# One order for five engines, rewritten: a pipelined two-layer gated block on one core

## Chip, core and metric

One NeuronCore of a Trainium2 chip runs the whole program. The metric is the device time of one execution in microseconds. The engines are named as in the profile: PE (TensorE, matmuls; PEld is its weight load), DVE (VectorE), ACT (ScalarE), POOL (GpSimd) and SP (SyncE, which only issues DMAs here).

## What is computed

64 samples of `x` (256 rows of 256) go through two gated cross-attention blocks and two gated feed-forward blocks against a context of 120 rows. All in float32. Products with a split operand are done in three fp32r passes (hi by hi, hi by lo, lo by hi).

```python
x = x + tanh(g_xattn[0]) * L0_xattn(ctx, ctx, layernorm(x))   # A: softmax over the 16 heads
x = x + tanh(g_ffn[0])   * L0_ffn(layernorm(x))               # B: silu(gate) * up, then down
x = x + tanh(g_xattn[1]) * L1_xattn(layernorm(x), ctx)        # C: one key/value head, softmax over keys
x = x + tanh(g_ffn[1])   * L1_ffn(layernorm(x))               # D: one 256x256 product with a bias
```

## The kernel before

The four steps are called A, B, C and D. A sample goes through all of them in seven loop passes: pass t makes the layernorm and transposes of A for sample t, the scores of A for t-1 and t-2, B for t-3, C over the passes behind that and D for t-6. So six passes lie in a straight-line front, 58 in a hardware loop `Fori` on each of the five engines, and six in a straight-line tail. The order of instructions on every engine is written out by hand, one list an engine, and what passes between engines is ordered by semaphores (`wait_ge` before, `then_inc` behind an instruction); each counts one up a pass.

What comes on PE in a pass, and what each writes: `scores0(c)` the scores of A for one half c of the queries, into the four `scores` banks of PSUM; `key_scores(c)` the scores of C from which only the maxima are taken, `scores1(cc)` those of C with the maxima subtracted, both into the same four banks; `attended0`, `attended1` the sums over values; `transposes(bank, st)` the transposed layernorm of step st; `queries`, `keys0`, `values0`, `keys_values1` the projections; `rows_out` the output products `wo0` (A), `wo1` (C) and `f1` (D); `gate_up(bank, m)` and `down(bank, m)` the six slices of B. All but the scores go through four work banks W[0] to W[3], one PSUM bank each, and every writer waits for the last reader of its bank. `keep_busy(bank, n)` issues n matmuls whose result nobody reads, fillers for stretches in which PE waits; they stand in the front and the tail only.

What hangs on them: DVE takes `head_max(c)` over the scores, subtracts it in two halves (`subtract_max`), ACT makes the two exponentials, POOL adds the heads (`add_heads`, `heads_total`, the last result is `z`), DVE takes `reciprocal0` and multiplies (`normalise`). `key_max(c)` on DVE makes the maxima of C; PE transposes them, ACT copies them to `mT`, and four small DMAs (`maxima_rows`) bring them into `qm1`, for which `scores1(0)` waits (`max_rows`). For B, ACT makes `tanh(m)`, DVE `gated(m)` and `hidden(m)` into two alternating buffers, ACT `hidden_hi(m)`, POOL `hidden_lo(m)`. For C, DVE's `queries_to_rows`, `reciprocal1`, `weigh` and `queries_to_columns` lead from `attended1` to `y1f`, split by ACT (`yC_hi`) and POOL (`yC_lo`). A layernorm is `moments` on DVE (two statistics, a wait for them, a small copy, two aggregates), `root` on POOL (four instructions, the last writes `shift`), `ln_apply` on ACT (two), `transposes` on PE, a copy and a rounding on ACT, and the low part on POOL or DVE.

The order on PE in a pass of the loop before: wo1, queries C, down 3 to 5, key_scores(1), transposes D, wo0, values0, key_scores(0), queries A, f1, transposes B, scores0(1), maxima, keys0, transposes A, gate_up 0 to 2, scores1(0), gate_up 3 and 4, scores1(1), attended1(0), gate_up 5, scores0(0), attended1(1), attended0 twice, transposes C, down 0 and 1, keys_values1, down 2 (lines 2460 to 2531). DVE's loop begins between the two subtractions of c=0 (line 1782). The lines that the prediction names: L1488, L1491, L1493 the parts of `moments`; L1517 `head_max`; L1523 `subtract_max`; L1511 `hidden`; L1531 `reciprocal0`; L1538 `queries_to_rows`; L402 to L408 `root`; L857 the exponentials; L814 `ln_apply`; L2175 transposes; L2218 `key_scores`; L2229 `scores0`; L2239 `scores1`; L2278 fillers.

## Times and profile before

| | |
|---|---|
| median of 3 runs | 2446.68 us (2445.35 to 2448.39) |
| profiled execution, its span | 2442.8 us |
| busy share of the span | PE 97%, DVE 90%, POOL 73%, ACT 70% |
| granted TensorE clock, mean | 0.996 |
| DMA | 73.26 MB, 30 GB/s |

The span is the time from the first to the last instruction of one profiled execution. A busy share is an average over the whole; where an engine waits, and for whom, is read in the timeline, which lists instructions with start, duration and, in square brackets, the idle time before them and what ended it. Matmuls overlap, so the time of a block of them is best read from one start to the next.

### The profile page before, as it was taken

The page shows a single profiled execution, that of the slowest core. Times are in us where ns is not written, and L with a number is a line of the kernel's source. Part 1 is how long each engine was busy: PE and PEld are TensorE (multiplying, and loading weights), DVE is VectorE, ACT ScalarE, POOL GpSimd, SP SyncE. Part 2 cuts the span into 40 slices and gives each one's busy share as a digit, 9 for nine tenths or more (in the row PEclk, how much of TensorE's full clock was granted, in tenths as well). Part 3 has the DMA queues.
Part 4 walks back from the last instruction along what each step waited for, and adds up shares of the span by engine and source line. Part 5 has one row for each costly group of instructions (what it writes and reads, how often), then busy time and mean ns, then how long its engine had stood idle before and what let it go on. Part 6 is the DMA issues. An engine that isn't in the chain of part 4 may idle for free.

```text
span 2442.8 us, 70142 instructions
## 1 busy us (share of the span) xinstructions
PE 2357.7 (97%) x27814; PEld 2081.6 (85%) x27814; DVE 2205.6 (90%) x3678; ACT 1719.5 (70%) x3402; POOL 1773.4 (73%) x2512
## 2 busy tenths in 40 slices
PE   6899999999999999999999999999999999999897
PEld 5788888888888888888888888888888888888786
DVE  6879999999999999999999999999999999999963
ACT  4567777777777777777777777777777777777664
POOL 3667777777777777787777777777777777777653
PEclk9999999999999999999999999999999999999999
DMA  3000010010011010011001000001001001101000
GB/s 106 25 19 29 28 35 24 28 35 24 28 35 30 22 35 30 26 31 30 28 28 30 28 28 31 28 28 35 24 28 35 24 28 35 30 22 35 17 19 15
DMA packets 74326, 73.26 MB, mean 30 GB/s; under 512 B 6555, under 2 KB 73393, under 8 KB 74290
## 3 DMA queue, kind: packets, MB, share of 16 engines
q1 hardware_dynamic: 74290, 72.75, 9.5%
q8 instruction: 26, 0.43, 0.1%
q14 instruction: 10, 0.08, 0.0%
HBM read 54.90 MB, written 16.78 MB: 29 GB/s over the span
## 4 chain that ended last, share of the span: by engine, by line
PE 64%; DVE 19%; ACT 7%; POOL 7%; issue 2%; DMA 0%; POOLq 0%; SPq 0%; DVEq 0%; ACTq 0%
PE work L2136 13%; PE work L2137 11%; PE work L2138 11%; DVE m L1517 6%; PE scores L2229 6%; PE scores L2239 5%; PE work L2272 5%; PE work L2175 4%; DVE scores L1523 4%; ACT e L857 3%; POOL zt L417 3%; PE scores L2218 3%; ACT xn_D L814 3%; PE work L2153 2%; PE work L2159 2%
## 5 line engine op out<-in xcount | busy, mean ns | idle before, releaser
L857 ACT ACTIVATE e<-scores 120x1024 f32<-120x1024 f32 x512 | 513.4, 1029 | 88.3 <-PE scores L2239 56.6
L2136 PE MATMUL work<-xt_hi_B,w_hi 128*128 128x256 f32 x1536 | 456.5, 297 | 3.8 <-DVE y_lo_A L1497 1.6
L2137 PE MATMUL work<-xt_lo_B,w_hi 128*128 128x256 f32 x1536 | 430.2, 280 | 0.0
L2138 PE MATMUL work<-xt_hi_B,w_lo 128*128 128x256 f32 x1536 | 430.0, 280 | 0.0
L417 POOL TENSOR_TENSOR zt<-e 120x512 f32<-120x512 f32 x256 | 328.7, 1285 | 118.1 <-ACT e L857 112.1
L411 POOL TENSOR_TENSOR h_lo<-h_f,h_hi 128x256 fp32r<-128x256 f32 x384 | 279.5, 735 | 147.3 <-ACT h_hi L807 147.1
L1517 DVE TENSOR_REDUCE m<-scores 120x128 fp32r<-120x2048 f32 x128 | 291.0, 2273 | 66.2 <-PE scores L2229 66.0
L2136 PEld LDWEIGHTS work<-xt_hi_B,w_hi 128*128 128x128 f32 x1536 | 289.3, 188 | 60.6 <-DVE h_f L1511 24.9
L1523 DVE TENSOR_TENSOR scores<-scores,m 120x1024 f32<-120x1024 f32 x256 | 302.8, 1227 | 4.3
L1535 DVE TENSOR_TENSOR e<-e,work 120x2048 f32<-120x2048 f32 x128 | 291.4, 2277 | 0.2
L2137 PEld LDWEIGHTS work<-xt_lo_B,w_hi 128*128 128x128 f32 x1536 | 289.9, 189 | 0.0
L2138 PEld LDWEIGHTS work<-xt_hi_B,w_lo 128*128 128x128 f32 x1536 | 289.3, 188 | 0.0
L1526 DVE TENSOR_REDUCE m<-scores 128x16 f32<-128x1920 f32 x128 | 275.4, 2152 | 5.8 <-PE scores L2218 4.9
L807 ACT ACTIVATE h_hi<-h_f 128x256 fp32r<-128x256 f32 x384 | 160.6, 419 | 132.1 <-DVE h_f L1511 131.8
L2136 PE MATMUL work<-w_hi,h_hi 128*128 128x256 f32 x768 | 224.3, 292 | 0.6 <-DVE x L1554 0.6
L2137 PE MATMUL work<-w_lo,h_hi 128*128 128x256 f32 x768 | 213.2, 278 | 0.0
L2138 PE MATMUL work<-w_hi,h_lo 128*128 128x256 f32 x768 | 212.9, 277 | 0.0
L607 POOL TENSOR_TENSOR y_lo_C<-y1f,y_hi_C 128x512 fp32r<-128x512 f32 x58 | 73.9, 1274 | 165.6 <-ACT y_hi_C L807 165.6
L814 ACT ACTIVATE xn_B<-x,shift_B,rstd_B 128x256 f32<-128x256 f32 x128 | 70.1, 595 | 158.8 <-POOL shift_B L408 158.8
L851 ACT ACTIVATE th<-work 128x256 f32<-128x256 f32 x384 | 150.7, 393 | 31.3 <-PE work L2138 14.2
L1508 DVE SCALAR_TENSOR_TENSOR act_g<-th,work 128x256 f32<-128x256 f32 x384 | 157.3, 410 | 9.9 <-ACT th L851 9.8
L421 POOL TENSOR_TENSOR zt<-zt 120x512 f32<-120x512 f32 x128 | 165.4, 1292 | 0.8
(256 smaller groups left out, 7283.5 us busy)
## 6 DMA issues: line engine op xcount, KB each, us to landing
x_ln<-xp SPq DMA_DIRECT2D x64, 256.0 KB, 2.7
x_res<-xp SPq DMA_DIRECT2D x64, 256.0 KB, 2.7
y<-y_out SPq DMA_DIRECT2D x64, 256.0 KB, 2.2
ctx_f_A<-cp SPq DMA_DIRECT2D x64, 128.0 KB, 2.5
ctx_f_C<-cp SPq DMA_DIRECT2D x64, 128.0 KB, 2.0
qm<-mT SPq DMA_DIRECT2D x256, 4.0 KB
e<-wi SPq DMA_DIRECT2D x3, 768.0 KB, 5.5
w_ctx<-wc SPq DMA_DIRECT2D x1, 656.0 KB
```

Source lines behind the costliest of these rows:

```text
L411: return pool.tensor_tensor(h_lo[:, m, :], h_f[:, m % 2, :], h_hi[:, m, :].bitcast(F32), ALU.subtract)
L417: return pool.tensor_tensor(zt[0:SC, c, 4 * h:4 * h + 4, :], e0[0:SC, c, 2 * h, :, :], e0[0:SC, c, 2 * h + 1, :, :], ALU.add)
L421: pool.tensor_tensor(zt[0:SC, c, 0:4, :], zt[0:SC, c, 0:4, :], zt[0:SC, c, 4:8, :], ALU.add)\
L807: return act.activation(out, src, ACT.Copy)
L857: return act.activation(e[0:SC, c, 2 * h:2 * h + 2, :, :].rearrange("p a b n -> p (a b n)"), scores[0:SC, 2 * h:2 * h + 2, :].rearrange("p ...
L1517: return dve.tensor_reduce(m0[0:SC, c, :], scores[0:SC, :, :].rearrange("p r (h n) -> p n (r h)", n=P), AX.X, ALU.max)
L1523: return dve.tensor_tensor(banks, banks, row, ALU.subtract)
L1526: return dve.tensor_reduce(m1[:, c, :].rearrange("p (r x) -> p r x", r=RG)[:, :, 0:4], scores[:, :, :].rearrange("p r (h n) -> p r h n", n ...
L1535: return dve.tensor_tensor(e, e, bank[0:SC, 0:P].unsqueeze(1).to_broadcast([SC, H, P]), ALU.mult)
L2136: pe.matmul(out, a_hi, b_hi_, start=first, stop=False, skip_group_check=parts)
L2137: pe.matmul(out, a_hi, b_lo_, start=False, stop=False, skip_group_check=parts)
L2138: last = pe.matmul(out, a_lo, b_hi_, start=False, stop=end, skip_group_check=parts)
```

## The change

All five orders are rewritten, in the front, in the loop and in the tail. The work is the same: the same products, the same elementwise instructions, the same 58 passes in the loop. What differs:

- The loop begins at another place of the cycle: on PE at `scores1(1)` instead of `wo1`, on DVE at `gated(3)`, on ACT at `tanh(4)`, on POOL at `hidden_lo(3)`. The front ends there and the tail begins there.
- `moments` is split into `bn_moments` and `aggregate`, each with its place in the order. For C the aggregates come after the next `head_max(1)`; the small copy reads `ident` instead of the statistics, and for C it is left out.
- The blocks of a pass use other work banks, so other bank waits stand before them.
- On SP the two loads of x stand together at the start of a pass, and `load_ctx("C")` behind `load_ctx("A")`.
- Fillers: 137 in the front and 121 in the tail before; 97 and 188 after. All but one group of the tail write a work bank that holds nothing in use.

The loops of before are printed above. Of the diff, this is the split and the five new loops (ACT's in part), then the end of PE's tail:

```diff
-DEPTH = 6
+LEAD = 6
+TAIL = 0
...
-            def moments(st, x, t):
-                for i in range(NT):
-                    last = dve.bn_stats(stats[st][:, i, :], x[:, i, :])
-                last.then_inc(s[f"ln_mom_{st}"], 1)
-                dve.wait_ge(s[f"ln_mom_{st}"], within(0, 1, t))
-                dve.tensor_copy(ln_count[:, :], stats[st][:, 0, 0:1])
-                for i in range(NT):
-                    last = dve.bn_aggr(mv[st][:, i, :], stats[st][:, i, :])
-                return last
+            def bn_moments(st, x):
+                for i in range(NT):
+                    last = dve.bn_stats(stats[st][:, i, :], x[:, i, :])
+                return last
+
+            def aggregate(st):
+                for i in range(NT):
+                    last = dve.bn_aggr(mv[st][:, i, :], stats[st][:, i, :])
+                return last
...
+with nc.sync.Fori(FIRST + LEAD, LAST + 1 - TAIL) as t:
+    load_x_ln(t)
+    load_x_res(t - 3)
+    sp.wait_ge(s["v0_mm"], t)
+    load_ctx("A", t - 1)
+    load_ctx("C", t - 4)
+    sp.wait_ge(s["mT_out"], t)
+    maxima_rows()
+    sp.wait_ge(s["res_D"], t)
+    store_y(t - 6)
...
+with nc.gpsimd.Fori(FIRST + LEAD, LAST + 1 - TAIL) as t:
+    pool.wait_ge(s["G_hi"], nth(3, 6, t - 1))
+    hidden_lo(3).then_inc(s["G_lo"], 1)
+    pool.wait_ge(s["yC_hi"], t)
+    pool.tensor_tensor(y_lo["C"][:, :, :], y1f[:, :, :], y_hi["C"][:, :, :].bitcast(F32), ALU.subtract)\
+    .then_inc(s["yC_lo"], 1)
+    pool.wait_ge(s["G_hi"], nth(4, 6, t - 1))
+    hidden_lo(4).then_inc(s["G_lo"], 1)
+    pool.wait_ge(s["T_hi_C"], t)
+    pool.tensor_tensor(xt_lo["C"][:, :, :], xt["C"][:, :, :], xt_hi["C"][:, :, :].bitcast(F32), ALU.subtract)\
+    .then_inc(s["T_lo_C"], 1)
+    hidden_lo(5).then_inc(s["G_lo"], 1)
+    pool.wait_ge(s["ln_eps_D"], t)
+    root("D", t - 6).then_inc(s["ln_rstd_D"], 1)
+    pool.wait_ge(s["ld_x_res"], 16 * t)
+    add_row(x_res, x_res, 0).then_inc(s["dn_add_res"], 1)
+    pool.wait_ge(s["A0_exp"], 2 * t)
+    add_heads(0, 1).then_inc(s["A0_zb"], 1)
+    pool.wait_ge(s["ln_eps_A"], t)
+    root("A", t).then_inc(s["ln_rstd_A"], 1)
+    pool.wait_ge(s["T_hi_D"], t)
+    pool.tensor_tensor(xt_lo["D"][:, :, :], xt["D"][:, :, :], xt_hi["D"][:, :, :].bitcast(F32), ALU.subtract)\
+    .then_inc(s["T_lo_D"], 1)
+    pool.wait_ge(s["ln_eps_B"], t)
+    root("B", t - 3).then_inc(s["ln_rstd_B"], 1)
+    add_heads(0, 0).then_inc(s["dn_heads_00"], 1)
+    pool.wait_ge(s["T_hi_B"], t)
+    pool.tensor_tensor(xt_lo["B"][:, :, :], xt["B"][:, :, :], xt_hi["B"][:, :, :].bitcast(F32), ALU.subtract)\
+    .then_inc(s["T_lo_B"], 1)
+    pool.wait_ge(s["dn_heads_00"], t)
+    heads_total(0, t - 2).then_inc(s["A0_z"], 1)
+    pool.wait_ge(s["A1_exp"], nth(0, 2, t))
+    add_heads(1, 0)
+    pool.wait_ge(s["A1_exp"], 2 * t)
+    add_heads(1, 1).then_inc(s["A1_zb"], 1)
+    pool.wait_ge(s["G_hi"], nth(0, 6, t))
+    hidden_lo(0).then_inc(s["G_lo"], 1)
+    pool.wait_ge(s["A1_zb"], t)
+    heads_total(1, t - 2).then_inc(s["A1_z"], 1)
+    pool.wait_ge(s["G_hi"], nth(1, 6, t))
+    hidden_lo(1).then_inc(s["G_lo"], 1)
+    pool.wait_ge(s["G_hi"], nth(2, 6, t))
+    hidden_lo(2).then_inc(s["G_lo"], 1)
+    add_row(x3_biased, x3, 1).then_inc(s["dn_add_x3"], 1)
+    root("C", t - 4).then_inc(s["ln_rstd_C"], 1)
+    pool.wait_ge(s["dn_add_x3"], t)
+    last_residual(x3_biased).then_inc(s["res_D"], 1)
...
+with nc.scalar.Fori(FIRST + LEAD, LAST + 1 - TAIL) as t:
+    act.wait_ge(s["G_mm"], nth(4, 6, t - 1))
+    tanh(4, W[3]).then_inc(s["G_tanh"], 1)
...
+    values1_out(W[1]).then_inc(s["dn_v1_out"], 1)
+    act.wait_ge(s["T_mm_C"], t)
+    act.activation(xt["C"][:, :, :], two(W[0], KC), ACT.Copy).then_inc(s["T_out_C"], 1)
+    keys1_even(W[1]).then_inc(s["dn_k1_even"], 1)
+    hidden_hi(4).then_inc(s["G_hi"], 1)
+    hidden_hi(5).then_inc(s["G_hi"], 1)
+    act.wait_ge(s["T_out_C"], t)
+    split_hi(xt_hi["C"][:, :, :], xt["C"][:, :, :]).then_inc(s["T_hi_C"], 1)
+    keys1_odd(W[1]).then_inc(s["kz1_odd"], 1)
+    act.wait_ge(s["A0_sub_dve"], nth(0, 2, t))
+    exponential(e0, 0, 0).then_inc(s["A0_exp"], 1)
+    act.wait_ge(s["A0_sub_dve"], 2 * t)
+    exponential(e0, 0, 1).then_inc(s["A0_exp"], 1)
+    split_hi(y_hi["A"][:, :, :], two(W[3], KC)).then_inc(s["yA_hi"], 1)
+    act.wait_ge(s["res_C"], t)
+    act.activation(x2_before[:, :, :], x2[:, :, :], ACT.Copy).then_inc(s["x2_before"], 1)
+    act.wait_ge(s["q_mm_C"], t)
+    query_out("C", W[1]).then_inc(s["q_out_C"], 1)
+    act.wait_ge(s["ln_rstd_D"], t)
+    ln_apply("D", x3).then_inc(s["ln_D"], 1)
...
+with nc.vector.Fori(FIRST + LEAD, LAST + 1 - TAIL) as t:
+    dve.wait_ge(s["G_tanh"], nth(3, 6, t - 1))
+    dve.wait_ge(s["G_h"], nth(1, 6, t - 1))
+    gated(3, W[0]).then_inc(s["G_a"], 1)
+    dve.wait_ge(s["A1_z"], t - 1)
+    dve.wait_ge(s["G_h"], nth(2, 6, t - 1))
+    reciprocal0(W[2], 1).then_inc(s["A1_rz"], 1)
+    dve.wait_ge(s["G_tanh"], nth(4, 6, t - 1))
+    gated(4, W[3]).then_inc(s["G_a"], 1)
+    dve.wait_ge(s["G_a"], nth(3, 6, t - 1))
+    dve.wait_ge(s["G_lo"], nth(1, 6, t - 1))
+    hidden(3, W[0]).then_inc(s["G_h"], 1)
+    dve.wait_ge(s["G_a"], nth(4, 6, t - 1))
+    dve.wait_ge(s["G_lo"], nth(2, 6, t - 1))
+    hidden(4, W[3]).then_inc(s["G_h"], 1)
+    dve.wait_ge(s["yz0_mm"], t)
+    queries_to_rows(0, W[1]).then_inc(s["yz0"], 1)
+    normalise(W[2], 1).then_inc(s["A1_p"], 1)
+    dve.wait_ge(s["yz1_mm"], t)
+    queries_to_rows(1, W[1]).then_inc(s["yz1"], 1)
+    dve.wait_ge(s["G_tanh"], 6 * (t - 1))
+    gated(5, W[0]).then_inc(s["G_a"], 1)
+    dve.wait_ge(s["yz1"], t)
+    reciprocal1().then_inc(s["rz1"], 1)
+    dve.wait_ge(s["G_a"], 6 * (t - 1))
+    dve.wait_ge(s["G_lo"], nth(3, 6, t - 1))
+    hidden(5, W[0]).then_inc(s["G_h"], 1)
+    dve.wait_ge(s["rz1"], t)
+    weigh().then_inc(s["y_weighed"], 1)
+    dve.wait_ge(s["y_weighed"], t)
+    queries_to_columns().then_inc(s["yC"], 1)
+    dve.wait_ge(s["A0_mm"], t)
+    head_max(0).then_inc(s["A0_max"], 1)
+    dve.wait_ge(s["A0_max"], t)
+    subtract_max(0, 0).then_inc(s["A0_sub_dve"], 1)
+    subtract_max(0, 1).then_inc(s["A0_sub_dve"], 1)
+    dve.wait_ge(s["woC_mm"], t)
+    residual(x3, x2_before, W[0]).then_inc(s["res_C"], 1)
+    dve.wait_ge(s["res_C"], t)
+    bn_moments("D", x3).then_inc(s["ln_mom_D"], 1)
+    dve.wait_ge(s["ln_mom_D"], t)
+    dve.tensor_copy(ln_count[:, :], ident[:, 0:1])
+    aggregate("D").then_inc(s["ln_eps_D"], 1)
+    dve.wait_ge(s["yA_hi"], t)
+    low(y_lo["A"][:, :, :], two(W[3], KC), y_hi["A"][:, :, :]).then_inc(s["yA_lo"], 1)
+    dve.wait_ge(s["ld_x_ln"], 16 * t)
+    bn_moments("A", x_ln).then_inc(s["ln_mom_A"], 1)
+    dve.wait_ge(s["ln_mom_A"], t)
+    dve.tensor_copy(ln_count[:, :], ident[:, 0:1])
+    aggregate("A").then_inc(s["ln_eps_A"], 1)
+    dve.wait_ge(s["x2_before"], t)
+    dve.wait_ge(s["dn_mm"], 6 * t)
+    residual(x2, x1, W[2]).then_inc(s["res_B"], 1)
+    dve.wait_ge(s["M1_mm"], t)
+    key_max(1).then_inc(s["M1_max"], 1)
+    dve.wait_ge(s["dn_add_res"], t)
+    dve.wait_ge(s["res_B"], t)
+    dve.wait_ge(s["woA_mm"], t)
+    residual(x1, x_res, W[1]).then_inc(s["res_A"], 1)
+    dve.wait_ge(s["res_A"], t)
+    bn_moments("B", x1).then_inc(s["ln_mom_B"], 1)
+    dve.wait_ge(s["ln_mom_B"], t)
+    dve.tensor_copy(ln_count[:, :], ident[:, 0:1])
+    aggregate("B").then_inc(s["ln_eps_B"], 1)
+    dve.wait_ge(s["M0_mm"], t)
+    key_max(0).then_inc(s["M0_max"], 1)
+    bn_moments("C", x2).then_inc(s["ln_mom_C"], 1)
+    dve.wait_ge(s["v0_mm"], t)
+    values0_out(W[1]).then_inc(s["v0_pad"], 1)
+    dve.wait_ge(s["A1_mm"], t)
+    dve.wait_ge(s["ln_mom_C"], t)
+    head_max(1).then_inc(s["A1_max"], 1)
+    aggregate("C").then_inc(s["ln_eps_C"], 1)
+    dve.wait_ge(s["A1_max"], t)
+    subtract_max(1, 0).then_inc(s["A1_sub_dve"], 1)
+    subtract_max(1, 1).then_inc(s["A1_sub_dve"], 1)
+    dve.wait_ge(s["G_tanh"], nth(0, 6, t))
+    gated(0, W[0]).then_inc(s["G_a"], 1)
+    transposed_lo("A", W[1]).then_inc(s["T_lo_A"], 1)
+    dve.wait_ge(s["G_a"], nth(0, 6, t))
+    hidden(0, W[0]).then_inc(s["G_h"], 1)
+    dve.wait_ge(s["A0_z"], t)
+    dve.wait_ge(s["T_lo_A"], t)
+    reciprocal0(W[1], 0).then_inc(s["A0_rz"], 1)
+    dve.wait_ge(s["G_tanh"], nth(1, 6, t))
+    gated(1, W[3]).then_inc(s["G_a"], 1)
+    dve.wait_ge(s["G_tanh"], nth(2, 6, t))
+    gated(2, W[2]).then_inc(s["G_a"], 1)
+    dve.wait_ge(s["G_a"], nth(1, 6, t))
+    hidden(1, W[3]).then_inc(s["G_h"], 1)
+    normalise(W[1], 0).then_inc(s["A0_p"], 1)
+    dve.wait_ge(s["G_a"], nth(2, 6, t))
+    dve.wait_ge(s["G_lo"], nth(0, 6, t))
+    hidden(2, W[2]).then_inc(s["G_h"], 1)
...
+with nc.tensor.Fori(FIRST + LEAD, LAST + 1 - TAIL) as t:
+    pe.wait_ge(s["T0_exp"], 2 * (t - 1))
+    scores1(1).then_inc(s["T1_mm"], 1)
+    pe.wait_ge(s["A0_p"], t - 1)
+    attended1(W[1], 0).then_inc(s["yz0_mm"], 1)
+    pe.wait_ge(s["G_h"], nth(3, 6, t - 1))
+    gate_up(W[0], 5).then_inc(s["G_mm"], 1)
+    pe.wait_ge(s["T1_exp"], 2 * t)
+    pe.wait_ge(s["yz0"], t)
+    attended1(W[1], 1).then_inc(s["yz1_mm"], 1)
+    attended0(W[3], 0).then_inc(s["yA0_mm"], 1)
+    scores0(0).then_inc(s["A0_mm"], 1)
+    pe.wait_ge(s["A1_p"], t)
+    attended0(W[3], 1).then_inc(s["yA1_mm"], 1)
+    pe.wait_ge(s["ld_ctx_C"], 16 * (t - 1))
+    pe.wait_ge(s["yz1"], t)
+    keys_values1(W[1]).then_inc(s["kv1_mm"], 1)
+    pe.wait_ge(s["ln_C"], t)
+    pe.wait_ge(s["G_h"], 6 * (t - 1))
+    transposes(W[0], "C").then_inc(s["T_mm_C"], 1)
+    down(W[2], 0).then_inc(s["dn_mm"], 1)
+    down(W[2], 1).then_inc(s["dn_mm"], 1)
+    pe.wait_ge(s["T_out_C"], t)
+    pe.wait_ge(s["yC_lo"], t)
+    rows_out(W[0], y_hi["C"], y_lo["C"], "wo1", False).then_inc(s["woC_mm"], 1)
+    down(W[2], 2).then_inc(s["dn_mm"], 1)
+    down(W[2], 3).then_inc(s["dn_mm"], 1)
+    pe.wait_ge(s["kz1_odd"], t)
+    pe.wait_ge(s["T_lo_C"], t)
+    queries(W[1], "C", "q1", False).then_inc(s["q_mm_C"], 1)
+    down(W[2], 4).then_inc(s["dn_mm"], 1)
+    pe.wait_ge(s["G_lo"], 6 * (t - 1))
+    down(W[2], 5).then_inc(s["dn_mm"], 1)
+    pe.wait_ge(s["q_out_C"], t)
+    key_scores(1).then_inc(s["M1_mm"], 1)
+    pe.wait_ge(s["ln_D"], t)
+    pe.wait_ge(s["yA_lo"], t)
+    transposes(W[3], "D").then_inc(s["T_mm_D"], 1)
+    rows_out(W[1], y_hi["A"], y_lo["A"], "wo0", False).then_inc(s["woA_mm"], 1)
+    pe.wait_ge(s["T_out_D"], t)
+    queries(W[3], "A", "q0", False).then_inc(s["q_mm_A"], 1)
+    pe.wait_ge(s["M1_max"], t)
+    key_scores(0).then_inc(s["M0_mm"], 1)
+    pe.wait_ge(s["res_A"], t)
+    values0(W[1]).then_inc(s["v0_mm"], 1)
+    pe.wait_ge(s["T_lo_D"], t)
+    rows_out(W[2], xt_hi["D"], xt_lo["D"], "f1", False).then_inc(s["f1_mm"], 1)
+    pe.wait_ge(s["ln_B"], t)
+    transposes(W[0], "B").then_inc(s["T_mm_B"], 1)
+    pe.wait_ge(s["M0_max"], t)
+    scores0(1).then_inc(s["A1_mm"], 1)
+    pe.wait_ge(s["T_out_B"], t)
+    maxima_transposed(W[0]).then_inc(s["mT_mm"], 1)
+    pe.wait_ge(s["ld_ctx_A"], 16 * t)
+    keys0(W[2]).then_inc(s["k0_mm"], 1)
+    pe.wait_ge(s["v0_pad"], t)
+    transposes(W[1], "A").then_inc(s["T_mm_A"], 1)
+    pe.wait_ge(s["mT_out"], t)
+    pe.wait_ge(s["T_lo_B"], t)
+    gate_up(W[0], 0).then_inc(s["G_mm"], 1)
+    pe.wait_ge(s["q_out_A"], t)
+    gate_up(W[3], 1).then_inc(s["G_mm"], 1)
+    pe.wait_ge(s["kz0_odd"], t)
+    gate_up(W[2], 2).then_inc(s["G_mm"], 1)
+    pe.wait_ge(s["max_rows"], 64 * t)
+    pe.wait_ge(s["A1_exp"], 2 * t)
+    scores1(0).then_inc(s["T0_mm"], 1)
+    pe.wait_ge(s["G_h"], nth(0, 6, t))
+    gate_up(W[0], 3).then_inc(s["G_mm"], 1)
+    pe.wait_ge(s["G_h"], nth(1, 6, t))
+    gate_up(W[3], 4).then_inc(s["G_mm"], 1)
...
+pe.wait_ge(s["yC_lo"], LAST + 6)
+rows_out(W[0], y_hi["C"], y_lo["C"], "wo1", False).then_inc(s["woC_mm"], 1)
+pe.wait_ge(s["f1_out"], LAST + 5)
+keep_busy(W[1], 37)
+pe.wait_ge(s["ln_D"], LAST + 6)
+transposes(W[0], "D").then_inc(s["T_mm_D"], 1)
+pe.wait_ge(s["f1_out"], LAST + 5)
+keep_busy(W[1], 22)
+pe.wait_ge(s["T_lo_D"], LAST + 6)
+rows_out(W[0], xt_hi["D"], xt_lo["D"], "f1", False).then_inc(s["f1_mm"], 1)
```

## Rows read from the trace of the kernel before

**Rows 1.** The page: its first line and busy times of the engines.
```profile
span 2442.8 us, 70142 instructions
PE 2357.7 (97%) x27814; PEld 2081.6 (85%) x27814; DVE 2205.6 (90%) x3678; ACT 1719.5 (70%) x3402; POOL 1773.4 (73%) x2512
```

**Rows 2.** Windows of the span: length, then busy time per engine, clock, DMA.
```profile
27.10:140.70 113.60, 94.09 (x1042) 85.63 (x1041) 89.70 (x125) 54.76 (x109) 62.37 (x88) 0.95 0.08 23
140.70:185.80 45.10, 42.67 (x472) 37.65 (x472) 34.99 (x70) 31.00 (x63) 31.55 (x49) 0.96 0.11 31
185.80:2255.20 2069.40, 2043.35 (x24511) 1811.77 (x24510) 1940.44 (x3250) 1518.87 (x3021) 1574.83 (x2223) 1.00 0.09 29
2255.20:2442.80 187.60, 162.74 (x1757) 137.64 (x1756) 121.60 (x202) 104.04 (x201) 100.75 (x136) 0.99 0.05 16
...
1217.60:1253.90 36.30, 35.84 (x432) 31.77 (x431) 34.04 (x58) 26.65 (x54) 27.64 (x40) 1.00 0.09 29
```

**Rows 3.** Timeline of PE, one pass: start, duration, engine, line, operation.
```profile
1202.53 1.15 PE L2239 MATMUL scores<-qm,km 32*128 32x256 f32 x16
...
1222.61 1.09 PE L2218 MATMUL scores<-kz,qm 32*128 32x240 f32 x16
1224.17 0.66 PE L2175 MATMUL work<-ident,xn_D 128*128 128x128 f32 x4 [0.46 <-ACT xn_D L814]
...
1231.49 1.17 PE L2229 MATMUL scores<-qt_A,kz 32*128 32x128 f32 x32
...
1238.84 1.15 PE L2239 MATMUL scores<-qm,km 32*128 32x256 f32 x16
...
1245.00 0.39 PE L2136 MATMUL work<-xt_hi_B,w_hi 128*128 128x256 f32 x1
```

**Rows 4.** Timeline of DVE, from the maximum of A1 to the statistics of D.
```profile
1232.73 2.29 DVE L1517 TENSOR_REDUCE m<-scores 120x128 fp32r<-120x2048 f32 x1 [1.05 <-PE scores L2229]
1235.06 2.36 DVE L1523 TENSOR_TENSOR scores<-scores,m 120x1024 f32<-120x1024 f32 x2
...
1243.55 0.96 DVE L1531 RECIPROCAL work<-z 120x128 f32<-120x128 f32 x1 [0.17 <-POOL z L427]
1244.42 0.41 DVE L1511 TENSOR_TENSOR h_f<-work,act_g 128x256 f32<-128x256 f32 x1
...
1248.85 0.72 DVE L1538 STREAM_TRANSPOSE yz_q<-work 128x512 f32<-128x512 f32 x1 [0.24 <-PE work L2272]
...
1253.86 2.37 DVE L1523 TENSOR_TENSOR scores<-scores,m 120x1024 f32<-120x1024 f32 x2
...
1256.85 0.75 DVE L1488 BATCH_NORM_STATS2 stats_D<-x 128x6 f32<-128x256 f32 x2
1257.63 0.15 DVE L1491 COPY ln_count<-stats_D 128x1 f32<-128x1 f32 x1
1257.70 0.24 DVE L1493 BATCH_NORM_AGGREGATE mv_D<-stats_D 128x2 f32<-128x6 f32 x2
```

**Rows 5.** Timeline of POOL: root of D, its first and its last instruction.
```profile
1258.02 0.20 POOL L402 TENSOR_TENSOR var_eps_D<-mv_D,eps_tile 128x2 f32<-128x2 f32 x1 [0.50 <-DVE mv_D L1493]
...
1259.10 0.19 POOL L408 TENSOR_TENSOR shift_D<-neg_mean_D,rstd_D 128x2 f32<-128x2 f32 x1
```

**Rows 6.** Timeline of ACT: exponentials of c=0 and the layernorm of D.
```profile
1255.12 2.16 ACT L857 ACTIVATE e<-scores 120x1024 f32<-120x1024 f32 x2
...
1259.33 1.09 ACT L814 ACTIVATE xn_D<-x,shift_D,rstd_D 128x256 f32<-128x256 f32 x2
```

**Rows 7.** SP's issue of the context of A, and its time to landing.
```profile
1227.74 0.34 SPq L283 DMA_DIRECT2D ctx_f_A<-cp  x1
...
ctx_f_A<-cp SPq DMA_DIRECT2D x1, 128.0 KB, 2.4
```

**Rows 8.** Timeline of PE in the tail: the last `attended1` and a group of fillers.
```profile
2421.16 1.07 PE L2272 MATMUL work<-e,v_one 120*32 120x256 f32 x16 [0.37 <-ACT e L857]
2422.16 2.76 PE L2278 MATMUL scores<-w_hi 128*128 128x256 f32 x21
```

2720 lines of the change are left out of this document (1297 added, 1423 removed), and 15 rows, old and new, of tables (given, passing).

## Prediction, written before the changed kernel was run

> **What bounds the kernel now.** I read the page first: PE is busy 97% of a span of 2442.8 us, DVE 90% [rows 1]. That says which engine is full, not what each pass waits for, so I cut the span at the starts of `scores1(0)` (called T0 here; its maxima come by DMA from `mT`). The front up to the first T0 takes 113.6 us from its first real block, the step from there to the first T0 inside the loop 45.1 us, 57 loop passes 2069.4 us (36.30 us each), and the rest from the last T0 of the loop 187.6 us [rows 2]. Together with 27.1 us of weight set-up they make the span. The profiled execution is 3.9 us shorter than the median of the runs, 2446.7; that lies around the span and stays.
>
> In the loop every pass repeats: T0 starts at 1202.53 and at 1238.84 [rows 3], clock 1.00, which is 2.4 GHz, and PE busy 35.84 of 36.30 us [rows 2]. The timeline of PE has one hole in it: `transposes(W[3], "D")`, T_D below, starts at 1224.17 although `key_scores(1)` before it (M1) started at 1222.61 and holds PE for 1.02 us until something else could start. Its row shows 0.46 us idle behind `xn_D`; by start times it is 0.54 [rows 3]. So PE's own need is about 36.30 - 0.54 = 35.76 us a pass, and 0.54 us are a chain that goes round. Followed back: `xn_D` on ACT starts at 1259.33, when POOL has `shift_D` (1259.10 + 0.19); POOL's root D starts at 1258.02, and DVE's second aggregate ends at 1257.94 [rows 4 to 6]. Before that DVE works almost without a hole back to `head_max(1)` at 1232.73, which had waited for the scores A1 (PE 1231.49 + 1.17) [rows 3, 4]. And from T_D PE needs 1231.49 - 1224.17 = 7.32 us to the start of A1. This circle, A1, DVE, root D, `ln_D`, T_D, PE, A1, is the 36.30 us.
>
> **The loop after the change.** PE gets the same blocks in nearly the same cyclic order; the loop only starts elsewhere (at `scores1(1)` instead of `wo1`). So the question is what happens on that circle.
>
> First stretch, `head_max(1)` to `hidden(3)`, which `gate_up(W[0], 5)` (g5) waits for. Before, `hidden(3)` starts at 1244.42 and ends at 1244.83; g5 starts at 1245.00 [rows 3, 4], just after it. The new order puts the aggregates of C between `head_max(1)` and the subtractions: two instructions of 0.12 started back to back cost about 0.15, of which 0.04 replace the wait for its own maximum, so the exponentials of c=1, POOL's sums and `reciprocal0(·, 1)`, which already waits 0.17 for POOL's `z`, come 0.11 later: 1243.66 instead of 1243.55. It also puts `gated(4)` (0.33 from start to start) in front of `hidden(3)`. End: 1244.83 + 0.11 + 0.33 = 1245.27, and g5 starts about 0.1 later, at 1245.37, so PE gets a new hole of 0.37 us here. It isn't yet a longer pass: it takes the place of the hole before T_D.
>
> Second stretch, `hidden(3)` to the aggregate of D on DVE: before 1257.94 - 1244.42 = 13.52 us. Out of it go `gated(4)` (0.33), the idle 0.24 us behind `yz1_mm`, since `normalise` now lies in front of the second transpose [rows 4], and one wait on its own previous instruction, since `gated(5)` now lies between the second transpose and `reciprocal1` (0.12). Left 12.83 from 1244.86: 1257.69, so 0.25 earlier than before. Then root D with its wakeup (1259.29 - 1257.94 = 1.35) and `ln_D` (1.09 + about 0.1): T_D at 1260.23, against 1224.17 + 36.30 = 1260.47.
>
> What an own-engine wait costs is read from the rows: COPY starts 0.03 after the end of the statistics it waits for (1256.85 + 0.75 = 1257.60, then 1257.63), the aggregate behind it 0.08 before COPY has ended [rows 4]; so 0.11. The Trainium skill, "VectorE: DVE Perf Modes", section "The DRAIN you can't avoid", says that the semaphore costs nothing extra. By that page the 0.12 above would be zero and T_D would come at 1260.35; the trace decides otherwise.
>
> Do ACT and PE let T_D start then? g5 at 1245.37 plus the blocks from g5 to M1 (1222.61 + 36.30 - 1245.00 = 13.91, less 0.1 because `keys_values1` no longer interrupts `down`) gives M1 at 1259.18 and T_D at 1260.2: PE arrives just then. ACT has, behind T_C, `xt_C`, keys, two splits and then the two exponentials, 2.16 us for the pair before [rows 6], `y_hi_A`, `x2_before` and `query_out("C")`, which the new order puts last: I get 1259.1 for `q_out_C` and M1 at 1259.2. Three chains meet within 0.1 us, which is why I don't give the loop more than this. From T_D on, PE has the same blocks, 7.32 us. New pass: 36.30 - 0.2 = **36.1 us**. The floor is PE's 35.75. Upwards nothing reasons a bound away: each of the three chains has a term of 0.1 to 0.3 that I set from neighbours (the aggregates, wakeups, where POOL's `hidden_lo(3)` falls), so 36.6.
>
> **What is moved for nothing, and its cover.** `load_x_ln` and `load_x_res` move behind `store_y`: needed over 8 us later, landing takes under 3. `load_ctx("A")` is issued after `v0_mm` as before, but values0 now comes behind M0, and only f1 (1.5), T_B (0.5), A1 (1.1) and the maxima (0.3), 3.4 us, lie between it and `keys0`. The load takes 2.4 from issue [rows 7], plus 0.2 before and at most 0.35 of issue: 0.5 us of cover remain (before, over 3). `load_ctx("C")` follows it on SP and costs nothing, being needed a half pass later. POOL has `add_row(x3)`, root C and the last residual (3.8 us) in front of `hidden_lo(3)`, which `hidden(5)` needs; by the row order it ends 0.1 us before DVE asks. If either cover goes, the pass grows by what is missing.
>
> The loop's branch now falls between `hidden(2)` and `gated(3)`, two DVE instructions of 0.4 us; before, it fell between two subtractions. The pair across the branch takes 2.37 us (1253.86), the pair in mid pass 2.36 (1235.06) [rows 4]: nothing is seen. That doesn't show a short instruction as cover, so I leave up to 0.2 us a pass in the upper end. The Trainium skill, "Runtime: NRT & Kernel Launch", section "Instruction fetch mechanics", warns that a taken branch whose target is outside the fetched pages stalls the engine; no row here shows one.
>
> **The ends.** PE blocks are counted from the code: 10.7 us of them move from front to tail, because the loop starts 11 us earlier in the cycle. Cut at T0 this drops out. Front to the first T0: the order gives 6 us more blocks, but gate_up of the first batch begins after four score rounds instead of six, and 97 fillers stand in the front instead of 137 (21 of them take 2.76 us [rows 8], so 0.12 each from start to start, 4.9 us less). I take 140.7 unchanged, with -8 to +6. The first step, 45.1 us before, is 8.8 over a pass; PE idles there while ACT finishes exponentials between T0 and T1 (42.67 busy of 45.10 [rows 2]). Now g3 and g4 lie between them as in the loop: I take 38.1. Tail: 187.6 us for some 140 us of blocks. Going by the new order, with a score round at about 5.8 us from scores to the last exponential, the T0 intervals come out near 38, 40, 36, 26, 20 and 28: 189, so +1.4, with -8 to +10; 188 fillers instead of 121 speak for longer holes there. The last chain, `yz1` to the store, keeps its steps, and of its fillers (22, 37 and 22) the 37 take 4.5 us where DVE, POOL and ACT need about 4.6 from `wo1` to `xn_D`, so they hide in the waits in which they lie.
>
> Sum: 140.7 + 38.1 + 57 × 36.1 + 189.0 = 2425.5, and 3.9 around it: **2429 us**, 17 less than the median: loop -11, first step -7, tail +1.
>
> **Rivals.** (a) PE's floor: the hole before g5 doesn't appear (POOL's `z` earlier, aggregates hidden) and T_D's is gone, 35.75 to 35.8 a pass: 57 × 0.33 = 19 less, 2410. For it: PE has no other hole; against it: the sum of DVE above. Chance 0.20. (b) Slower: `hidden(3)` becomes the bound. If `gated(4)` must wait for its tanh, or `z` comes 0.3 later than I have it, g5's hole adds straight to the circle, since DVE behind it has no idle time left to take up: 36.6 a pass, +28 us, 2458. It decides from a hole of about 0.5 before g5. The missing cover of `keys0` would look the same in time. Chance 0.20. (c) The order changes and the circle does not: 36.3 a pass with the ends unchanged, 2446; or the loop as forecast and a tail 12 us longer, 2441. Chance 0.15. Forecast: 0.45, own range 2419 to 2440.
>
> **Numbers.** Leaving out a tenth on each side, (a) reaches down to 2404 and (b) up to 2456. A measurement of this kernel can tell about 0.2% from no change. Faster by over 0.2% (below 2441.8): 0.45 of the forecast less 0.02, 0.20 of (a) and 0.05 of (c), 0.68. Within 0.2%: 0.12. Slower: 0.20.
>
> **What would show it.** Right: T0 to T0 36.0 to 36.2; the hole before T_D under 0.1 and one of 0.2 to 0.4 before g5; DVE's idle behind `yz1_mm` gone; a first step near 38. (a): no hole before g5. (b): a hole of over 0.5 before g5, or `keys0` waiting for DMA. Wrong would be a loop bound at a place that I have not named, or ends off by over 10 us.

## Result and profile after

The changed kernel takes 2410.36 us (median, 2408.7 to 2411.3) against 2446.01 us of the kernel before on the same chip: ratio 0.9853, 95% interval 0.9838 to 0.9867, 35.7 us less. The forecast was 2429. The sign was right and the gain was twice the forecast one. The time lies inside the wide range (2404 to 2456) and outside the forecast's own (2419 to 2440); it is what rival (a) had as its number. The profiled executions are 2442.8 and 2407.6 us long, so 35.2 us can be placed in the two traces.

The page of the changed kernel: span, busy times, and the first line of the chain that ended last.

```profile
span 2407.6 us, 70477 instructions
PE 2356.7 (98%) x27841; PEld 2082.5 (86%) x27841; DVE 2185.2 (91%) x3596; ACT 1727.5 (72%) x3402; POOL 1771.7 (74%) x2512
PE 93%; DVE 4%; ACT 1%; POOL 1%; issue 1%; DMA 0%; SPq 0%; POOLq 0%; DVEq 0%; ACTq 0%
```

Before, the same first line of the chain read:

```profile
PE 64%; DVE 19%; ACT 7%; POOL 7%; issue 2%; DMA 0%; POOLq 0%; SPq 0%; DVEq 0%; ACTq 0%
```

This is the change in one view: the chain that ended last went over DVE, POOL and ACT once a pass (the circle of the prediction), and now it stays on PE nearly throughout. It leaves PE only where a row shows idle time, though, and the wait of 0.1 us before g5 (below) shows none in the matmul rows; so this view does not say that PE alone sets the pass.

Windows of the changed kernel with the cuts of [rows 2]: front, first step, 57 passes, tail, then one pass. Columns: length, busy time of PE, PEld, DVE, ACT and POOL, granted clock, DMA.

```profile
27.10:132.60 105.50, 92.52 (x1042) 84.85 (x1040) 90.45 (x131) 59.26 (x118) 65.02 (x98) 0.95 0.10 28
132.60:168.80 36.20, 35.88 (x431) 31.82 (x430) 32.99 (x56) 26.87 (x55) 24.17 (x35) 1.00 0.05 15
168.80:2222.60 2053.80, 2045.44 (x24512) 1812.20 (x24510) 1923.73 (x3193) 1526.10 (x3022) 1573.71 (x2224) 1.00 0.10 30
2222.60:2407.60 185.00, 168.08 (x1823) 144.74 (x1822) 118.52 (x188) 104.46 (x200) 104.06 (x141) 1.00 0.06 20
...
1206.30:1242.30 36.00, 35.84 (x434) 31.75 (x433) 33.71 (x57) 26.73 (x54) 27.61 (x39) 1.00 0.09 30
```

| us | before | after | measured | forecast |
|---|---|---|---|---|
| front to the first T0 | 113.6 | 105.5 | -8.1 | 0 |
| first step | 45.1 | 36.2 | -8.9 | -7 |
| 57 passes | 2069.4 | 2053.8 | -15.6 | -11 |
| tail | 187.6 | 185.0 | -2.6 | +1 |

Half of the gain is outside the loop. The largest part of what the forecast lacked, 8.1 of 17.9 us, is in the front, which it took as unchanged.

Timeline of PE in one pass of the changed kernel, the rows that answer to [rows 3]:

```profile
1206.24 1.17 PE L2297 MATMUL scores<-qt_A,kz 32*128 32x128 f32 x32
1213.67 1.15 PE L2307 MATMUL scores<-qm,km 32*128 32x256 f32 x16
1218.83 1.07 PE L2340 MATMUL work<-e,v_one 120*32 120x256 f32 x16
1219.93 0.39 PE L2204 MATMUL work<-xt_hi_B,w_hi 128*128 128x256 f32 x1
1233.94 1.09 PE L2286 MATMUL scores<-kz,qm 32*128 32x240 f32 x16
1234.96 0.66 PE L2243 MATMUL work<-ident,xn_D 128*128 128x128 f32 x4
1242.29 0.95 PE L2297 MATMUL scores<-qt_A,kz 32*128 32x128 f32 x24
```

T_D starts 1.02 us behind M1 (before 1.56 in [rows 3]); that hole is gone. g5 starts 1.10 behind `attended1(0)`, where it was 1.00: the new hole there is 0.1 and not 0.37. What g5 waits for stands in the row of its weight load (PEld), `hidden(3)` on DVE (line 1509):

```profile
1219.93 0.19 PEld L2204 LDWEIGHTS work<-xt_hi_B,w_hi 128*128 128x128 f32 x1 [0.51 <-DVE h_f L1509]
```

Timeline of DVE in the same pass, answering to [rows 4]:

```profile
1207.48 2.29 DVE L1515 TENSOR_REDUCE m<-scores 120x128 fp32r<-120x2048 f32 x1 [0.83 <-PE scores L2297]
1209.69 0.24 DVE L1491 BATCH_NORM_AGGREGATE mv_C<-stats_C 128x2 f32<-128x6 f32 x2
1209.84 2.34 DVE L1521 TENSOR_TENSOR scores<-scores,m 120x1024 f32<-120x1024 f32 x2
...
1217.38 0.42 DVE L1509 TENSOR_TENSOR h_f<-work,act_g 128x256 f32<-128x256 f32 x1
1217.72 0.42 DVE L1506 SCALAR_TENSOR_TENSOR act_g<-th,work 128x256 f32<-128x256 f32 x1
1218.27 0.96 DVE L1529 RECIPROCAL work<-z 120x128 f32<-120x128 f32 x1
1219.14 0.41 DVE L1506 SCALAR_TENSOR_TENSOR act_g<-th,work 128x256 f32<-128x256 f32 x1
1219.46 0.74 DVE L1509 TENSOR_TENSOR h_f<-work,act_g 128x256 f32<-128x256 f32 x2
...
1222.93 0.70 DVE L1536 STREAM_TRANSPOSE yz_q<-work 128x512 f32<-128x512 f32 x1
1223.55 0.38 DVE L1506 SCALAR_TENSOR_TENSOR act_g<-th,work 128x256 f32<-128x256 f32 x1
1223.86 0.34 DVE L1539 RECIPROCAL rz_q<-yz_q 128x32 f32<-128x32 f32 x1
...
1231.95 0.24 DVE L1491 BATCH_NORM_AGGREGATE mv_D<-stats_D 128x2 f32<-128x6 f32 x2
```

From the start of `head_max(1)` to the end of the aggregate of D: 1232.19 - 1207.48 = 24.71 us; before 1257.94 - 1232.73 = 25.21. DVE's part of the circle is 0.50 us shorter, and the pass only 0.28.

### The profile page after: what moved, and what is told of

It reads as the page before. It is cut to its first block, busy times and chain, and to the rows that moved or that the text cites. A ratio compares the mean times of both kernels' runs of the same rounds, so it can differ in the third digit from the quotient of the medians.

```text
span 2407.6 us, 70477 instructions
## 1 busy us (share of the span) xinstructions
PE 2356.7 (98%) x27841; PEld 2082.5 (86%) x27841; DVE 2185.2 (91%) x3596; ACT 1727.5 (72%) x3402; POOL 1771.7 (74%) x2512
## 4 chain that ended last, share of the span: by engine, by line
PE 93%; DVE 4%; ACT 1%; POOL 1%; issue 1%; DMA 0%; SPq 0%; POOLq 0%; DVEq 0%; ACTq 0%
PE work L2204 19%; PE work L2205 17%; PE work L2206 17%; PE scores L2307 6%; PE scores L2297 6%; PE scores L2286 5%; PE work L2340 5%; PE work L2327 5%; PE work L2243 5%; PE work L2227 3%; PE work L2221 2%; PE work L2233 2%; PE work L2320 1%; PE work L2236 1%; DVE m L1524 1%
## 5 line engine op out<-in xcount | busy, mean ns | idle before, releaser
L858 ACT ACTIVATE e<-scores 120x1024 f32<-120x1024 f32 x512 | 504.5, 1030 | 86.5 <-PE scores L2307 70.1
L2204 PE MATMUL work<-xt_hi_B,w_hi 128*128 128x256 f32 x1536 | 449.7, 293 | 14.0 <-POOL xt_lo_B L496 2.0
L2204 PE MATMUL work<-w_hi,h_hi 128*128 128x256 f32 x768 | 218.3, 284 | 0.0
L808 ACT ACTIVATE h_hi<-h_f 128x256 fp32r<-128x256 f32 x384 | 153.9, 420 | 35.5 <-DVE h_f L1509 35.5
L576 POOL TENSOR_TENSOR xt_lo_B<-xt_B,xt_hi_B 128x512 fp32r<-128x512 f32 x58 | 73.7, 1271 | 133.2 <-ACT xt_hi_B L808 133.2
L1506 DVE SCALAR_TENSOR_TENSOR act_g<-th,work 128x256 f32<-128x256 f32 x384 | 150.8, 406 | 11.8 <-ACT th L852 11.8
```

The source lines that it names most:

```text
L808: return act.activation(out, src, ACT.Copy)
L858: return act.activation(e[0:SC, c, 2 * h:2 * h + 2, :, :].rearrange("p a b n -> p (a b n)"), scores[0:SC, 2 * h:2 * h + 2, :].rearrange("p ...
L2204: pe.matmul(out, a_hi, b_hi_, start=first, stop=False, skip_group_check=parts)
```

## Experiments

Each ran beside the kernel before on the same chip. The pass of each is the distance from T0 to T0 over the 57 loop passes of its trace: 36.31 us before, 36.03 after. For the loop, the same intervals between starts on PE were read from every trace, as medians over some 33 passes in its middle; they add up to the pass within 0.03.

| interval, us | before | after | b_dve | a_pe4 | a_dve | a_dve2 | a_g4 | a_both | a_h5 |
|---|---|---|---|---|---|---|---|---|---|
| T0 to attended1(0) | 5.16 | 5.16 | 5.17 | 5.16 | 5.16 | 5.16 | 5.16 | 5.16 | 5.16 |
| attended1(0) to g5 | 1.00 | 1.10 | 1.00 | 1.11 | 1.09 | 1.10 | 1.00 | 1.00 | 1.00 |
| g5 to M1 | 13.92 | 14.00 | 13.91 | 14.00 | 14.00 | 14.24 | 14.13 | 14.05 | 14.03 |
| M1 to T_D | 1.55 | 1.02 | 1.88 | 1.59 | 1.11 | 1.03 | 1.03 | 1.03 | 1.15 |
| T_D to A1 | 7.33 | 7.33 | 7.33 | 7.27 | 7.32 | 7.32 | 7.32 | 7.32 | 7.33 |
| A1 to T0 | 7.34 | 7.43 | 7.35 | 7.43 | 7.43 | 7.43 | 7.43 | 7.43 | 7.43 |
| pass | 36.31 | 36.03 | 36.64 | 36.58 | 36.11 | 36.26 | 36.05 | 36.02 | 36.10 |

### What sets the pass: a little more for PE, a little more for DVE

```diff
 # PE's loop (b_pe4: W[0], a_pe4: W[1])
 key_scores(1).then_inc(s["M1_mm"], 1)
+keep_busy(W[0], 4)
```

> The kernel before, with four more matmuls on PE in the loop, right behind key_scores(1), where PE waits 0.54 us for xn_D; nobody reads their result. Four of them take about 0.5 us (21 of them 2.76 in the tail). Theory (before's pass is set by the circle A1, DVE, root D, ln_D, T_D, and PE has 0.54 us to spare there): the pass stays 36.3 us, the total within 5 us of before; the hole before T_D shrinks to nearly nothing. Rival (PE's own work sets the pass): 0.5 us a pass, +27 us.

> The changed kernel, with the same four matmuls behind key_scores(1) in the loop. Theory (its pass is set by PE, xn_D being ready 0.14 us before PE asks, so 0.1 us to spare at most): 0.4 to 0.5 us a pass, 23 to 27 us over the changed kernel, so 2433 to 2438 and about 0.995 of before. Rival (the circle still sets the pass, at a shorter length): nothing, 2410.

Measured: b_pe4 2449.15 us, ratio to before 1.0008 (0.9998 to 1.0018), pass 36.34. a_pe4 2440.67 us, 0.9975 (0.9964 to 0.9987), pass 36.58. Timeline of PE, b_pe4 first and then a_pe4, from M1 to T_D:

```profile
1225.74 1.09 PE L2218 MATMUL scores<-kz,qm 32*128 32x240 f32 x16
1226.76 0.74 PE L2278 MATMUL work<-w_hi 128*128 128x256 f32 x4
1227.34 0.61 PE L2175 MATMUL work<-ident,xn_D 128*128 128x128 f32 x4
```
```profile
1214.52 1.09 PE L2286 MATMUL scores<-kz,qm 32*128 32x240 f32 x16
1215.55 0.74 PE L2346 MATMUL work<-w_hi 128*128 128x256 f32 x4
1216.13 0.60 PE L2243 MATMUL work<-ident,xn_D 128*128 128x128 f32 x4
```

The two look alike and cost different things. In b_pe4 M1 to T_D goes from 1.55 to 1.60, 0.05 us for 0.58 us of matmuls: they lie in a hole that was there. In a_pe4 it goes from 1.02 to 1.59, all of it, and the pass by 0.55, 30 us in all, a little over the 23 to 27 expected. So before, the pass was set by a chain other than PE's list; after, PE's list from g5 to A1 is on the circle that sets it.

Between A1 and g5 that is not so. g5 waits 0.10 us for `hidden(3)`, so a circle is closed there through DVE and POOL: A1, `head_max(1)`, the exponentials and sums of c=1, `hidden(3)`, g5, and PE from g5 to A1. In the table it is 7.43 + 5.16 + 1.10 = 13.69 us from A1 to g5 and about 22.35 from there to A1. Without that wait PE would turn in 35.93, an estimate from the same table. The four matmuls lie on the part that both circles have in common, so a_pe4 can't tell them apart, and no run adds work to DVE between A1 and `hidden(3)`.

```diff
 # DVE's loop, ahead of the statistics of D (b_dve: ahead of moments)
+dve.tensor_reduce(spare[:, 0:1], x3[:, 0, :], AX.X, ALU.max)
 bn_moments("D", x3).then_inc(s["ln_mom_D"], 1)
```

> The kernel before, with one more DVE instruction in the loop ahead of the statistics of D: a maximum over 128x256 into one spare column, some 0.35 us, read by nobody. Theory (the circle through DVE sets the pass): the whole of it is added, 0.35 us a pass, +20 us. Rival (PE sets the pass): 0, as DVE has over 1 us of idle time in it.

> The changed kernel with the same extra DVE instruction of some 0.35 us ahead of the statistics of D. Theory (PE sets the pass, the circle through DVE is only 0.14 us behind it): 0.35 less 0.14, so about 0.2 us a pass or +12 us over the changed kernel, with a new hole of 0.2 before T_D. Rival A (the circle still sets it): +20 us. Rival B (DVE has room to spare): 0.

Measured: b_dve 2463.0 us, 1.0072 (1.0055 to 1.0089), pass 36.64: the instruction costs 0.33, and all of it appears between M1 and T_D (1.55 to 1.88). a_dve 2415.83 us, 0.9870 (0.9854 to 0.9887), pass 36.11: of the same 0.33 only 0.08 appear. The circle through T_D is therefore 0.25 us behind what sets the pass, not 0.14 as I had read from the end of `xn_D`; by itself it would turn in about 35.78.

```diff
 # DVE's loop of the changed kernel
+dve.tensor_reduce(spare[:, 0:1], x2[:, 0, :], AX.X, ALU.max)
 dve.wait_ge(s["yz1"], t)
 reciprocal1().then_inc(s["rz1"], 1)
```

> The changed kernel with the same extra DVE instruction (a maximum over 128x256 into a spare column, 0.35 us), but ahead of reciprocal1 instead of ahead of the statistics of D, so that y1f and the splits of C come later too. In the trace of the changed kernel y_lo_C ends 0.29 us before wo1 starts, and xn_D is 0.25 us early by the run with the instruction further down. Theory (PE sets the pass and two circles stand close behind it, one through T_D with 0.25 to spare, one through y_lo_C and wo1 with 0.1 to 0.2, a block's first weights being wanted some 0.1 ahead): 0.15 to 0.25 us a pass, 9 to 14 us over the changed kernel, with wo1 starting late. Rival (only the circle through T_D is close): 0.08 a pass as before, 5 us.

Measured: 2419.98 us, 0.9889 (0.9872 to 0.9907), pass 36.26. Seven microseconds higher in DVE's list the same instruction costs 0.23 a pass instead of 0.08, and not at T_D (1.03) but between g5 and M1 (14.00 to 14.24), where wo1 waits for `y_lo_C`. So another circle runs from DVE over `queries_to_columns`, the two splits and wo1 back into PE, with only 0.1 us to spare. The prediction did not have it.

### Edits that should free PE

```diff
 # a_g4, DVE's loop of the changed kernel
-dve.wait_ge(s["G_tanh"], nth(4, 6, t - 1))
-gated(4, W[3]).then_inc(s["G_a"], 1)
 dve.wait_ge(s["G_a"], nth(3, 6, t - 1))
 dve.wait_ge(s["G_lo"], nth(1, 6, t - 1))
 hidden(3, W[0]).then_inc(s["G_h"], 1)
+dve.wait_ge(s["G_tanh"], nth(4, 6, t - 1))
+gated(4, W[3]).then_inc(s["G_a"], 1)
 # a_merge, PE's loop of the changed kernel
-attended0(W[3], 0).then_inc(s["yA0_mm"], 1)
 scores0(0).then_inc(s["A0_mm"], 1)
+attended0(W[3], 0).then_inc(s["yA0_mm"], 1)
```

> The changed kernel with gated(4) and its wait behind hidden(3) on DVE instead of ahead of it, so that gate_up 5 on PE no longer starts right at the end of hidden(3). If PE sets the pass and what it loses before gate_up 5 is the 0.1 us that it waits for hidden(3), up to 0.1 us a pass, 6 us less than the changed kernel (2404). Rival (that start is set by attended1(0) anyway): 0. Second rival (hidden(4) comes later, and with it down(4)): slower by some us.

> The changed kernel with scores0(0) ahead of both attended0 on PE, as in the kernel before, instead of between them. If each change between kinds of block costs PE 0.05 to 0.1 us, 0.1 to 0.15 us a pass, 6 to 8 us less than the changed kernel (2403). Rival (PE's time is the sum of its blocks in any order, or the later values for y_hi_A cost ACT the same): 0.

> The changed kernel with both edits, gated(4) behind hidden(3) and both attended0 together. If PE sets the pass, the two gains add until the circle through DVE (0.14 us behind) takes over: at most 0.15 to 0.2 us a pass, 8 to 12 us less than the changed kernel, about 2400. Rival: the larger of the two alone, or 0.

Measured: 2411.88 us (0.9850, 0.9833 to 0.9867), 2410.98 us (0.9849, 0.9832 to 0.9865) and 2410.92 us (0.9847, 0.9831 to 0.9864): none can be told from the changed kernel (a_merge has a pass of 36.02). The rivals' time, no change, came each time, but for a_g4 not the rival's reason: the start of g5 was set by `hidden(3)`, for the edit takes the 0.1 us off (1.10 to 1.00). The interval behind it grows by 0.07 in half of the passes and by 0.14 in the others. By blocks, wo1 takes 1.36 us from start to start in the changed kernel and 1.46 in a_g4. PE arrives at it just when `y_lo_C` is there: it ends at 1227.59 in a_both, and wo1 starts at 1227.76 with 0.17 to its second matmul, where 0.12 is the step within a block.

That `y_lo_C` is late is the edit's own doing. `hidden(4)` now stands right behind `gated(4)`, whose result it needs, as DVE's rows in a_g4 show (`hidden(3)`, `gated(4)`, `hidden(4)`, `queries_to_rows(0)`):

```profile
1220.22 0.41 DVE L1509 TENSOR_TENSOR h_f<-work,act_g 128x256 f32<-128x256 f32 x1
1220.55 0.41 DVE L1506 SCALAR_TENSOR_TENSOR act_g<-th,work 128x256 f32<-128x256 f32 x1
1220.99 0.42 DVE L1509 TENSOR_TENSOR h_f<-work,act_g 128x256 f32<-128x256 f32 x1
1221.33 0.70 DVE L1536 STREAM_TRANSPOSE yz_q<-work 128x512 f32<-128x512 f32 x1
```

From `gated(4)` to `hidden(4)` are 0.44 us, where 0.33 lie between its neighbours. Counted from `head_max(1)`, `y_lo_C` ends after 20.56 us instead of 20.43: 0.13 later, on a circle with 0.10 to spare. So a_g4 gives no measure of what PE would need with g5 free.

> The changed kernel with gated(4) behind hidden(3), both attended0 together, and the transposes of C and down 0 and 1 ahead of keys_values1 on PE (the transposes' copy ahead of values1_out on ACT), which is the order of before there. In before this stretch from attended1(0) to key_scores(1) takes 14.92 us, in the changed kernel 15.10. If the order of the blocks is what costs PE, up to 0.15 us a pass, 8 us less than the changed kernel. If what costs it is that a block's first weights can't be loaded ahead when its operand comes just in time, it depends on which chain is late: 0, or slower where wo1 waits for the copy.

```diff
 # a_kv, on top of a_both: PE's loop, and the copy of the transposes ahead of values1_out on ACT
-keys_values1(W[1]).then_inc(s["kv1_mm"], 1)
 transposes(W[0], "C").then_inc(s["T_mm_C"], 1)
 down(W[2], 0).then_inc(s["dn_mm"], 1)
 down(W[2], 1).then_inc(s["dn_mm"], 1)
+keys_values1(W[1]).then_inc(s["kv1_mm"], 1)
```

Measured: 2456.32 us, 1.0042 (1.0027 to 1.0057), pass 36.82. A miss. PE has one long wait in a pass:

```profile
1218.78 0.36 PE L2204 MATMUL work<-xt_hi_C,w_hi 128*128 128x256 f32 x1 [0.52 <-POOL xt_lo_C L558]
```

ACT now waits for `keys_values1` with `xt_hi_C` queued behind it, and the queries of C wait for its low part. Putting one block where it had stood before, without the order on ACT that went with it, costs more than the whole loop gained.

```diff
 # a_h5, on top of a_both: DVE's loop
-dve.wait_ge(s["G_a"], 6 * (t - 1))
-dve.wait_ge(s["G_lo"], nth(3, 6, t - 1))
-hidden(5, W[0]).then_inc(s["G_h"], 1)
 dve.wait_ge(s["rz1"], t)
 weigh().then_inc(s["y_weighed"], 1)
 dve.wait_ge(s["y_weighed"], t)
 queries_to_columns().then_inc(s["yC"], 1)
+dve.wait_ge(s["G_a"], 6 * (t - 1))
+dve.wait_ge(s["G_lo"], nth(3, 6, t - 1))
+hidden(5, W[0]).then_inc(s["G_h"], 1)
```

> The changed kernel with gated(4) behind hidden(3), both attended0 together, and hidden(5) on DVE behind queries_to_columns instead of ahead of weigh, so that y1f comes 0.15 us earlier. If the 0.1 us that the first of these edits gained before gate_up 5 was given back at wo1 because y_lo_C was late, it is now kept: 35.9 us a pass, 6 us less than the changed kernel, about 2404. Rival (PE needs 36.0 whatever is ready, or down(5) now waits for hidden_lo(5)): 0 or some us more.

Measured: 2413.76 us, 0.9865 (0.9848 to 0.9883), pass 36.10. The first half of the expectation came: wo1 takes 1.36 again, so the gain at g5 is kept. But M1 to T_D goes to 1.15: `hidden(5)` no longer fills DVE's wait between `reciprocal1` and `weigh`, and the wait of `hidden(4)` for `gated(4)` is there too. From `head_max(1)` to the end of the aggregate of D are 24.99 us instead of 24.71. These 0.28 are more than the 0.25 to spare, and the circle through T_D is the last. In four of these five variants the pass stays between 36.02 and 36.10, in a_kv it gets much worse. No version tried beats the changed kernel.

### One line of DVE's order alone

```diff
 # b_norm, DVE's loop of the kernel before
-dve.wait_ge(s["A1_rz"], t)
-normalise(W[2], 1).then_inc(s["A1_p"], 1)
 dve.wait_ge(s["G_tanh"], nth(4, 6, t))
 gated(4, W[3]).then_inc(s["G_a"], 1)
 dve.wait_ge(s["yz0_mm"], t)
 queries_to_rows(0, W[1]).then_inc(s["yz0"], 1)
+dve.wait_ge(s["A1_rz"], t)
+normalise(W[2], 1).then_inc(s["A1_p"], 1)
```

> The kernel before with one step of DVE's loop moved as in the change: normalise(W[2], 1) comes behind queries_to_rows(0) instead of ahead of it, so that the second queries_to_rows no longer waits 0.24 us for attended1(1). If the gain of the loop is DVE's half of the circle, the aggregate of D comes 0.24 to 0.3 us earlier and so does T_D: 0.2 to 0.3 us a pass, 11 to 17 us less than before, most of the loop's gain of 15 from one moved line. Rival (the 0.24 turns up as a wait further down, or the whole order is needed): 0 to 5 us less.

Measured: 2614.97 us, 1.0683 (1.0665 to 1.0702), 166 us slower, a pass of 39.2 us, in the middle of the loop 38.6 and 39.8 about as often. The miss was large and plain in its timelines, DVE's first and then PE's:

```profile
1212.85 0.41 DVE L1511 TENSOR_TENSOR h_f<-work,act_g 128x256 f32<-128x256 f32 x1
1215.13 0.42 DVE L1508 SCALAR_TENSOR_TENSOR act_g<-th,work 128x256 f32<-128x256 f32 x1 [1.86 <-ACT th L851]
1215.46 0.71 DVE L1538 STREAM_TRANSPOSE yz_q<-work 128x512 f32<-128x512 f32 x1
1216.10 2.25 DVE L1535 TENSOR_TENSOR e<-e,work 120x2048 f32<-120x2048 f32 x1
```
```profile
1215.05 1.17 PE L2229 MATMUL scores<-qt_A,kz 32*128 32x128 f32 x32
1218.40 1.07 PE L2272 MATMUL work<-e,v_one 120*32 120x256 f32 x16 [2.18 <-DVE e L1535]
```

`normalise` had covered a wait of 1.9 us for tanh(4), which stood behind the exponentials of c=1 on ACT; and `attended1(1)` writes the bank that `normalise` reads. The changed kernel can have this order because ACT makes tanh(4) ahead of those exponentials and `attended1(1)` uses W[1]. So this line can't be moved alone: it needs ACT's order and the banks with it.

### The ends: order or fillers

> The kernel before without any of its fillers, in the front or the tail; they compute nothing that is read. If they only lie in waits and hold the clock up (they take 19.5 us of PE in the front and first step): the same waits at a lower clock, so 0 to 10 us more. If they stand in the way of blocks that could start sooner: up to 10 us less.

> The changed kernel without any of its fillers (13.3 us of PE in its front, and 188 in the tail). If the 17 us that front and first step lost come from the order of the blocks, the front up to the first T0 stays within 3 us of the changed kernel's 105.5, and 15 to 20 us below that of before without fillers. If they come from the other set of fillers (97 instead of 137, and the clock), the difference between the two kernels without fillers is below 8 us there. In the tail the 188 fillers are worth 0 to 10 us of clock.

The loop inside `keep_busy` runs `range(0)` in both. Measured: b_nofill 2463.1 us, 1.0076 (1.0058 to 1.0094); a_nofill 2420.92 us, 0.9898 (0.9880 to 0.9916). Windows by the same cuts, b_nofill, then a_nofill:

```profile
27.10:147.70 120.60, 86.73 (x911) 77.53 (x911) 89.92 (x128) 54.35 (x109) 62.64 (x90) 0.83 0.07 22
147.70:194.00 46.30, 43.79 (x474) 37.86 (x474) 34.98 (x70) 30.90 (x63) 31.48 (x50) 0.93 0.10 30
...
2264.10:2459.30 195.20, 156.06 (x1635) 129.82 (x1634) 121.57 (x201) 103.93 (x200) 100.47 (x135) 0.90 0.05 16
```
```profile
27.10:136.40 109.30, 87.32 (x953) 78.42 (x952) 91.54 (x133) 59.22 (x119) 65.22 (x98) 0.89 0.10 28
136.40:172.60 36.20, 35.87 (x431) 31.80 (x430) 32.99 (x56) 26.89 (x55) 24.20 (x35) 1.00 0.05 15
...
2228.00:2421.80 193.80, 156.73 (x1635) 131.86 (x1634) 118.45 (x188) 104.67 (x200) 103.87 (x141) 0.89 0.06 19
```

Front and first step together: 166.9 against 145.5, 21.4 us apart, where with fillers it is 158.7 against 141.7, 17.0 apart. So the gain there is the order's; the fillers of before narrow it, since they are worth 8.2 us there and those of after 3.8. The expectation had put the 15 to 20 us on the front alone: there it is 11.3, and the front without fillers is 3.8 over 105.5 where 3 was allowed, so it held only with the first step taken in. In the tail they are worth 7.6 and 8.8 us, at a granted clock of 0.99 and 1.00 with them, 0.90 and 0.89 without. I had given them 0 to 10 us; before's are worth 16 in all. The clock explains it, but no run holds the clock and takes the fillers away, so this stays argued.

```diff
 # a_late, PE's front of the changed kernel, ahead of the first gate_up
-keep_busy(W[3], 17)
+keep_busy(W[3], 57)
```

> The changed kernel with 57 instead of 17 fillers ahead of the first gate_up block of its front (at 71.5 us), some 5 us more of PE. If the front from there to the first T0 is bound by PE and the early gate_up is what shortened it, all 5 us are added to the total. If a chain through ACT, DVE or POOL bounds it (scores round by scores round), 0 to 2 us.

Measured: 2414.00 us, 0.9870 (0.9852 to 0.9887), 3.6 us over the changed kernel's median. In the profiled execution the first T0 comes at 139.0 instead of 132.65. With the same front, the first T0 of the other variants lies between 131.6 and 134.2, so 4.8 to 7.4 us appear there for 5 us of fillers, and 3.6 in the medians: nearer to the first expectation, though the medians leave room for some slack. So PE's list has little or no slack at this place. It doesn't follow that PE bounds what comes behind, since the score rounds stand behind the fillers in the same list and move with them: from the first `gate_up` to the first T0 are 61.3 us in a_late and 61.2 in the changed kernel, and in the chain that ended last PE has about 44% of that stretch in both, DVE, ACT and POOL most of the rest.

## Why the prediction was right or wrong

**The bound before: right.** The circle A1, DVE, root D, `ln_D`, T_D, PE was named as the 36.30 us, with 0.54 us free on PE. b_pe4 and b_dve show both: PE takes 0.58 us more at a cost of 0.03 a pass, and DVE's 0.33 are paid in full (16 us in the medians, 20 expected).

**First DVE stretch: one term too large.** `reciprocal0(·, 1)` was put 0.11 later because of the aggregates of C. From `head_max(1)` to it are 10.79 us after and 10.82 before. The aggregates do take their place, with 2.36 instead of 2.33 us from the maximum to the subtraction, but they cost 0.03, for they lie where DVE had waited for its own result; and the wait for `z` further down, 0.17 before, had room for the rest. `gated(4)` took its 0.32. So `hidden(3)` came 0.29 later and not 0.44. Before, g5 had started 0.17 behind its end, now it is 0.06, so g5 comes 0.18 later counted from A1; PE itself takes 0.09 more from A1 to T0, and 0.1 is left as the hole where 0.37 was forecast.

**Second DVE stretch: the signs right, one size off.** Counted from `reciprocal0` to the second `queries_to_rows`, 5.30 us became 4.66; `gated(5)`, 0.31, moved behind it, so the hole was worth 0.33. I had taken 0.24 for it, the idle time in brackets in [rows 4]; from start to start it is 1248.85 - 1248.21 - 0.31 = 0.33, by these rows of before (`gated(5)`, and `reciprocal1` behind the transpose of 1248.85):

```profile
1248.21 0.40 DVE L1508 SCALAR_TENSOR_TENSOR act_g<-th,work 128x256 f32<-128x256 f32 x1
1249.60 0.35 DVE L1541 RECIPROCAL rz_q<-yz_q 128x32 f32<-128x32 f32 x1
```

The wait of DVE on its own result was worth 0.13 where 0.12 was forecast: 0.75 us from the transpose to `reciprocal1` before, 0.62 to `gated(5)` now, which fills it. a_g4 opens such a wait between `gated(4)` and `hidden(4)` and pays 0.11 for it. The Trainium skill, "VectorE: DVE Perf Modes", section "The DRAIN you can't avoid", says that a semaphore between two DVE instructions costs nothing extra; these rows disagree. From `hidden(3)` to the end of the aggregate of D are 12.73 us, 0.79 less than before where 0.69 was forecast. With the 0.29 of the first stretch the circle lost 0.50 us and not 0.25.

**The new pass: right to 0.07 us, with luck.** 36.1 was forecast as three chains meeting, T_D, `q_out_C` and g5; it is 36.03. T_D is 0.25 behind by a_dve. The chain over g5 is the one that closes, and by the forecast's own numbers it gave 36.03: 13.88 from A1 to g5, 13.81 to M1, 1.02 and 7.32. Measured are 13.69, 14.00, 1.02 and 7.33: A1 to g5 was put 0.19 too long and g5 to M1 0.19 too short, and the two errors cancel. Rival (a) had nearly this time by "no hole before g5"; there is one, of 0.1, and T_D's is gone, so its condition was half met. Its floor of 35.75 was PE's time in the order of before, less the one hole. In the new order PE comes round 0.25 to 0.28 later than that: g5 waits 0.10 for `hidden(3)`, g5 to M1 is 0.08 longer although I had taken 0.1 off, and A1 to T0 0.09, net of 0.23 in front of g0, where PE waits for POOL's `xt_lo_B`, and 0.14 that g0 to g2 lost. These are no idle times of the kind that carry a bracket in the matmul rows. The rows of PE's weight loads show it at g0:

```profile
1208.40 0.47 PEld L2243 LDWEIGHTS work<-ident,xn_A 128*128 128x128 f32 x4
1209.20 0.19 PEld L2204 LDWEIGHTS work<-xt_hi_B,w_hi 128*128 128x128 f32 x1 [0.34 <-issue]
1209.31 0.19 PEld L2205 LDWEIGHTS work<-xt_lo_B,w_hi 128*128 128x128 f32 x1
```

A block whose operand is early follows the last one at the step of its matmuls, 0.12; one whose wait ends just in time begins with 0.17 to 0.23, since its first weights are loaded only then. The Trainium skill, "TensorE: Matmul & The Clock Gate", section "Step-by-step: what each phase is for", says that PE pulls a weight load ahead of matmuls in flight; the 1.36 and 1.46 us of wo1 agree with what is lost when it can't, though no run here isolates it. The three places named add up to 0.27 us a pass, nearly as much as the loop gained (0.28). What in g5 to M1 costs its 0.08 is not located; a_merge, which puts back the old order of one block there, has the same 14.0.

**What moved for nothing: right.** `keys0` follows the maxima by 0.28 us in the changed kernel, without a wait for its load; `hidden(5)` follows `reciprocal1` at once; and across the loop's branch on DVE, `hidden(2)` to `gated(3)`, there are 0.34 us (1217.38 to 1217.72), as between such instructions elsewhere. Rival (b) had its conditions in view, and none came.

**First step: right in kind, 1.9 us too long.** 36.2 for a forecast of 38.1: it is an ordinary pass now, and the clock there went from 0.96 to 1.00.

**Front: this is where the forecast failed.** Of the 17.9 us by which the sum of 2425.5 was too long, 8.1 are here, 4.0 in the tail, 3.9 in the loop and 1.9 in the first step. "I take 140.7 unchanged" set 6 us more blocks against an earlier `gate_up`, which it didn't price, and fewer fillers, which it put at 4.9 us less; measured is 132.6. A count would have done most of it. From 27.1 to the first T0 of the loop both kernels have the same real blocks: before, 1514 matmuls of which 137 are fillers; after, 1472 with 96 or 97.

```profile
27.10:185.80 158.70, 136.76 (x1514) 0.96 0.09 26
```
```profile
27.10:168.80 141.70, 128.40 (x1472) 0.96 0.09 25
```

The fillers take 19.5 us before and 13.3 after. So PE's time goes: real blocks 117.3 to 115.1, fillers 19.5 to 13.3, idle 21.9 to 13.3. Fillers lie in waits, so waiting, filled or not, went from 41.4 to 26.6 us: 14.8 of the 17.0 that front and first step lost together. Why the same real blocks take 2.2 us less is open. The first `gate_up` starts at 71.5 instead of 89.05, behind four score rounds instead of six, and from there on blocks of B stand where PE had waited for exponentials and normalised sums. a_late shows that PE has little slack at the start of this stretch, not what bounds the rest of it. The wait in front of each block is in the trace of before, and the new list says which block comes there: that sum was open to me. That the shorter waiting comes from these blocks is read from the order; no run puts the first `gate_up` back alone.

**Tail: put 1 us longer, came 2.6 us shorter.** T0 intervals 37.8, 39.0, 35.2, 24.4, 20.0 and 28.7 for 38, 40, 36, 26, 20 and 28. These forecasts add up to 188, not to the 189 of the sum. The same count as for the front gives the 2.6 us by which the tail is shorter than before: real blocks 144.4 to 143.0, and waiting, filled or not, 43.2 to 42.0 (the fillers take 18.3 and 25.1 us of PE). So the added fillers lie in waits and the tail's order won little. Apart from the fillers, worth 1.2 us more than before's, no run tests it.

## What to carry to other kernels

Find the circle that sets a pass, then measure how far the next ones are behind, by adding a known small piece to one engine at one place: the share of it that appears is the answer, and the same piece at two places of one list told two circles apart. Put one such piece on every stretch that could be the last: here DVE between A1 and `hidden(3)` was left out, and the wait at g5 stood only in the weight-load row. Once several circles meet, moving a single line gave nothing here, or opened a wait of its own (0.11 us in a_g4), or broke a cover, as `normalise` did for 166 us. For the straight-line ends, count the waiting, fillers included: a better order has that to win, and here it was as much as the loop gave.

## What was not expected of the hardware

A PE block whose operand comes just in time costs 0.1 us more than one whose operand is early (wo1 1.46 us in a_g4, 1.36 in the changed kernel), without an idle time in its matmul rows. A DVE instruction that needs the result of the one right before it starts 0.11 to 0.13 us later than one that doesn't (0.44 against 0.33 us, 0.75 against 0.62). And fillers are worth more than their look: without them the granted clock in the ends fell from 0.95 to 0.83 (front of before) and from 1.00 to 0.89 (tail of after), and the kernels were 16 and 10.5 us slower.
